# Four graph layers on one core: second layer with values stationary and probabilities scaled on GpSimd, and a changed order of work in the third and last layers

## The reference, cut to what matters

```python
h = maximum(layernorm(x), 0);  x = x + L0(h, adj, adj)   # attention, 8 heads of 32, eight masks, biases
h = maximum(layernorm(x), 0);  x = x + L1(h, adj)        # attention, 4 heads of 64, output bias only
h = maximum(layernorm(x), 0);  x = x + L2(h, adj)        # graph attention, 4 heads of 256, tanh, gated blend
h = maximum(layernorm(x), 0);  x = x + L3(h, adj)        # gated graph layer, 8 heads of 32, cosine links

def L1(x, mask):
    q, k, v = split_heads(x @ Wq), split_heads(x @ Wk), split_heads(x @ Wv)
    sim = where(mask, einsum('bhid,bhjd->bhij', q, k) / 8, -max)
    out = einsum('bhij,bhjd->bhid', softmax(sim), v)
    return merge_heads(out) @ Wo + bo

def L2(h, adj):
    Wh = einsum('bni,hoi->bhno', h, W) + bW
    A = tanh(where(adj, einsum('bhnp,bhmp->bhnm', einsum('bhno,hop->bhnp', Wh, attn), Wh), 0))
    ha = merge_heads(relu(einsum('bhnm,bhmo->bhno', A, Wh))) @ A_w.T
    hf = h @ fc_w.T
    c = sigmoid(hf @ g1_w.T + ha @ g2_w.T + gbias)
    return hf * c + ha * (1 - c)

def L3(x, m):                       # sm = mask, keep = not sm[..., 0:1]
    m = x @ map_w.T + map_b;  n = m by head / norm
    cos_adj = (n @ n.T * ~sm > 0.1)
    p = softmax(where(sm, -1e10, q @ k.T / sqrt(32))) * keep     # q, k from m
    adj = cos_adj * p
    return relu((adj @ sem) @ gcn_W.T / (adj.sum(-1) + 1))
```

## Time and profile before

| | |
|---|---|
| median of 3 runs | 2108.23 us (2107.6 to 2110.77) |
| the profiled execution | 2107.84 us, span 2106.0 us, granted PE clock 0.987 |
| PE busy | 2019.6 us (96%) |
| PE weight loads | 1865.0 us (89%), beside PE |
| DVE busy | 1486.2 us (71%) |
| ACT busy | 1019.4 us (48%) |
| POOL busy | 609.1 us (29%) |
| first, second, third, last layer | to about 385, 705, 1655, 2106 us |

### The profile page before, as it was taken

One profiled execution on the slowest core, in us unless ns is written; L12 is line 12 of the kernel. 1 busy time (PEld: TensorE's weight loads), 2 busy tenths in 40 slices (PEclk: granted clock), 3 DMA queues, 4 the chain that ended last, 5 costly groups with the idle time before them and its releaser, 6 DMA issues. The chain is left out here.

```text
span 2106.0 us, 52874 instructions
## 1 busy us (share of the span) xinstructions
PE 2019.6 (96%) x18448; PEld 1865.0 (89%) x18448; DVE 1486.2 (71%) x3280; ACT 1019.4 (48%) x2122; POOL 609.1 (29%) x656
## 2 busy tenths in 40 slices
PE   7999999899999799999999999999999899999998
PEld 7988888799999699999999999999998788888886
DVE  7999989577777455555555555555555599999998
ACT  6777777455555322322223223222222476776675
POOL 4545555322222011011111111111111344444443
PEclk9999999899999899999999999999999899999999
DMA  3222222433223200111111001110110122112221
GB/s 107 77 68 76 64 74 76 132 101 92 82 85 91 67 24 17 32 31 31 31 31 31 26 19 31 31 31 31 31 31 21 27 63 61 53 53 61 61 61 46
DMA packets 149370, 113.31 MB, mean 54 GB/s; under 512 B 42944, under 2 KB 148800, under 8 KB 149312
## 3 DMA queue, kind: packets, MB, share of 16 engines
q1 hardware_dynamic: 149312, 112.52, 18.3%
HBM read 78.93 MB, written 33.55 MB: 53 GB/s over the span
## 5 line engine op out<-in xcount | busy, mean ns | idle before, releaser
L274 POOL TENSOR_TENSOR ln_rstd<-ln_var_eps,minus_half 128x2 f32<-128x2 f32 x128 | 90.8, 709 | 760.4 <-DVE ln_var_eps L267 759.3
L1723 ACT ACTIVATE l_cat_hi<-banks 128x512 fp32r<-128x512 f32 x128 | 76.5, 598 | 260.2 <-PE banks L1894 260.2
L182 PE MATMUL banks<-ln_hT_hi,square_w_hi_held 128*128 128x256 f32 x512 | 153.2, 299 | 5.1 <-DVE square_w_lo_held L657 3.2
L291 ACT ACTIVATE ln_h<-ln_x,ln_shift,ln_rstd 128x256 f32<-128x256 f32 x256 | 139.1, 591 | 31.5 <-DVE ln_shift L281 26.8
L182 PE MATMUL banks<-ln_hT_hi,l_g_w_hi 128*128 128x256 f32 x512 | 148.8, 291 | 4.1 <-PEq L1992 4.1
L182 PE MATMUL banks<-l_cat_hi,l_aw_hi 128*128 128x256 f32 x512 | 144.5, 282 | 0.0
L183 PE MATMUL banks<-ln_hT_lo,square_w_hi_held 128*128 128x256 f32 x512 | 144.3, 282 | 0.0
L184 PE MATMUL banks<-ln_hT_hi,square_w_lo_held 128*128 128x256 f32 x512 | 144.0, 281 | 0.0
L184 PE MATMUL banks<-ln_hT_hi,l_g_w_lo 128*128 128x256 f32 x512 | 142.6, 278 | 0.0
L183 PE MATMUL banks<-ln_hT_lo,l_g_w_hi 128*128 128x256 f32 x512 | 142.5, 278 | 0.0
L183 PE MATMUL banks<-l_cat_lo,l_aw_hi 128*128 128x256 f32 x512 | 141.6, 277 | 0.0
(11 more groups left out here) (244 smaller groups left out, 6994.1 us busy)
## 6 DMA issues: line engine op xcount, KB each, us to landing
hidden<-y SPq DMA_DIRECT2D x96, 256.0 KB, 2.1
ln_x<-hidden SPq DMA_DIRECT2D x96, 256.0 KB, 2.7
x_res<-hidden SPq DMA_DIRECT2D x96, 256.0 KB, 2.9
ln_x<-x SPq DMA_DIRECT2D x32, 256.0 KB, 2.8
x_res<-x SPq DMA_DIRECT2D x32, 256.0 KB, 3.0
out<-y SPq DMA_DIRECT2D x32, 256.0 KB, 2.1
l_adj_u<-adj SPq DMA_DIRECT2D x96, 16.0 KB, 2.3
l_stage_attnT<-L_attnT SPq DMA_DIRECT2D x4, 256.0 KB, 3.2
```

The costliest lines, as they stand in the source:

```text
L182: nc.tensor.matmul(out, lhs(lh), rhs(rh), start=start, stop=False, skip_group_check=True)
L274: self.nc.gpsimd.tensor_tensor(self.rstd[:, g.slot], self.var_eps[:, g.slot], self.core.minus_half[:, 0:PAIRS], ALU.pow).then_inc(self.rst ...
L291: last = self.nc.scalar.activation(self.h[:, u, p, :], self.x[:, u, p, :], ACT.Relu, bias=self.shift[:, u, p:p + 1], scale=self.rstd[:, u, ...
L1723: nc.scalar.activation(cat_hi[:, h * KC:(h + 1) * KC], halves(B_HP[h]), ACT.Relu).then_inc(cat_hi_ready.sem, 1)
```

## The change

In the second layer the probabilities are scaled as in the first: DVE sums and inverts, POOL multiplies, PE transposes `weighted` and takes the values as the stationary operand, 128 columns wide, so the output transposes, `l_o` and the column of ones go. Here POOL's root is queued behind `weighted`; DVE's statistics come ahead of the softmax; PE's value projection is split around the transposes. In all layers the offset on line 267 becomes a `scalar_tensor_tensor` that takes the variance twice. In the third layer `Wh` is computed in units of 512 (two accumulations of 256), 256 and 260 columns, and `ha` in two halves in two banks. In the last layer DVE's order is another, POOL's mask comes last, and ACT applies the layer norm ahead of the second exponential.

```diff
@@ LayerNorm
+    def aggregate(self, dve, g, p):
+        u = g.slot
+        last = self.nc.vector.bn_aggr(self.mean_var[:, u, p, :], self.stats[:, u, p, :])
+        if p == PAIRS - 1:
+            last.then_inc(self.mean_var_ready.sem, 1)
+    def offset(self, dve, g):
         after(dve, self.mean_var_ready, g)
         after(dve, self.rstd_ready, g.back(2))
-        nc.vector.tensor_scalar(self.var_eps[:, u], self.mean_var[:, u, :, 1], LN_EPS, None,
-                                ALU.add).then_inc(self.var_eps_ready.sem, 1)
+        var = self.mean_var[:, u, :, 1]
+        self.nc.vector.scalar_tensor_tensor(out=self.var_eps[:, u], in0=var, scalar=LN_EPS, in1=var, op0=ALU.add,
+                                            op1=ALU.max).then_inc(self.var_eps_ready.sem, 1)
...
@@ attention_layer, POOL
-                if gn is not None:
+                if NT == 2 and gn is not None:
                     ln.root(pool, gn)
-                if direct and c2.exists(groups):
+                if c2.exists(groups):
                     for t in range(NT):
...
+                if NT == 1 and gn is not None:
+                    ln.root(pool, gn)
@@ attention_layer, DVE, one tile
+                    if gn is not None:
+                        ln.statistics(dve, gn, first=True)
                     if c2.exists(groups):
                         softmax_shift(0)
-                    if gn is not None:
-                        ln.statistics(dve, gn, first=True)
                     if e.exists(groups):
                         split_oT()
+                    if c2.exists(groups):
+                        weights_of_rows(0)
                     if gn is not None:
                         ln.statistics(dve, gn, first=False)
                         ln.shifts(dve, gn)
...
-                if not direct and c2.exists(groups):
-                    bank = ps[:, B_O:B_O + PAIRS, 0:heads * VW].rearrange("q p (h e) -> q p h e", h=heads)
...
@@ attention_layer, PE
-                if not direct and e.exists(groups):
-                    transpose_o()
                 if b1.exists(groups):
                     keys()
-                if not direct and c2.exists(groups):
-                    transpose_prob(prob, prob_ready, 0)
                 if e.exists(groups):
                     project_out()
                 if b1.exists(groups):
-                    values()
+                    values(range(PAIRS) if NT == 2 else range(1))
+                if c2.exists(groups):
+                    for t in range(NT):
+                        transpose_prob(t)
+                if NT == 1 and b1.exists(groups):
+                    values(range(1, PAIRS))
...
+                    for p in range(PAIRS):
+                        after(pe, probT_ready, c2, p // TP + 1)
+                        for b in range(2):
+                            for j in range(HH):
+                                r0, col = j * OUT_ROWS % P, j * OUT_ROWS // P * TOK + (2 * p + b) * S
+                                last = nc.tensor.matmul(
+                                    ps[r0:r0 + OUT_ROWS, B_OT, col:col + S], v_bd[:, u, p, b, j].rearrange("q a e -> q (a e)"),
+                                    probT[:, u, p // TP, (p % TP) * HH + j, b * S:(b + 1) * S], start=True, stop=True,
+                                    skip_group_check=True)
@@ graph_attention_layer
-    THIRDS = ((0, 320), (320, 384), (704, WC - 704))
+    UNITS = ((0, 512), (512, 256), (768, WC - 768))
-        B_HP, B_HA = (5, 6, 5, 6), 7
+        B_HP, B_HA = (5, 6, 5, 6), (7, 5)
...
-                    nc.scalar.activation(ha_hi[:], halves(B_HA), ACT.Copy).then_inc(ha_hi_ready.sem, 1)
+                    for c in range(KC):
+                        after(act, ha_in_psum, c2, c + 1)
+                        nc.scalar.activation(ha_hi[:, c], ha(c), ACT.Copy).then_inc(ha_hi_ready.sem, 1)
...
@@ gated_graph_layer, DVE (the calls alone)
                 softmax_shift(0); ln.statistics(dve, gn, first=True)
-                gate_output()                       # kept, den, r_den, factor, t
-                ln.statistics(dve, gn, first=False) # two aggregates, offset
-                softmax_shift(1)
-                ln.shifts(dve, gn)
-                n_bd copies; keep; sum_of_prob(0); m; sum_of_prob(1); link(0); link(1); norm_sq; norm_cl; y
+                gate_sums(); ln.aggregate(dve, gn, 0); gate_denominator(); ln.aggregate(dve, gn, 1)
+                gate_reciprocal(); ln.offset(dve, gn); gate_output()    # factor, t
+                ln.shifts(dve, gn)
+                softmax_shift(1)
+                n_bd copies; m; keep; link(0); norm_sq; norm_cl; link(1); sum_of_prob(0); sum_of_prob(1); y
@@ gated_graph_layer, ACT
-                    exponentials(1)
-                if gn is not None:
-                    ln.apply(act, gn)
+                if gn is not None:
+                    ln.apply(act, gn)
+                if c2.exists(groups):
+                    exponentials(1)
```

More of the change, by code:

```diff
@@ L508, in step @@
                 c2, e = g.back(2), g.back(3)
[L509 removed]
+                if low_on_pool and e.exists(groups):
                     after(pool, oT_hi_ready, e)
@@ L647, in step @@
                     ln.evacuate_hi(act, gn, B_HT)
-                if direct and b1.exists(groups):
+                if b1.exists(groups):
                     evacuate_v()
@@ L1204, in step @@
                     ln.root(pool, gn)
-                if g.exists(groups):
-                    after_dma(pool, adj_loaded, g)
-                    after(pool, scores_in_psum, g.back(2), apart=core)
-                    after(pool, keep_ready, g.back(2), apart=core)
-                    nc.gpsimd.tensor_scalar(mask[:, g.slot], adj_u8[:, g.slot], -MASKED, None,
-                                            ALU.mult).then_inc(mask_ready.sem, 1)
                 b1 = g.back(1)
@@ L1226, in step @@
                                             ALU.mult).then_inc(n_ready.sem, 1)
+                if g.exists(groups):
+                    after_dma(pool, adj_loaded, g)
+                    after(pool, scores_in_psum, g.back(2), apart=core)
+                    after(pool, keep_ready, g.back(2), apart=core)
+                    nc.gpsimd.tensor_scalar(mask[:, g.slot], adj_u8[:, g.slot], -MASKED, None,
+                                            ALU.mult).then_inc(mask_ready.sem, 1)
             run_steps(pool, step, groups, 1)
@@ L1369, in step @@
                 if e.exists(groups):
-                    gate_output()
-                if gn is not None:
-                    ln.statistics(dve, gn, first=False)
-                if c2.exists(groups):
-                    softmax_shift(1)
-                if gn is not None:
-                    ln.shifts(dve, gn)
+                    gate_sums()
+                if gn is not None:
+                    after(dve, ln.stats_ready, gn, apart=core)
+                    ln.aggregate(dve, gn, 0)
+                if e.exists(groups):
+                    gate_denominator()
+                if gn is not None:
+                    ln.aggregate(dve, gn, 1)
+                if e.exists(groups):
+                    gate_reciprocal()
+                if gn is not None:
+                    ln.offset(dve, gn)
+                if e.exists(groups):
+                    gate_output()
                 if c2.exists(groups):
@@ L1384, in step @@
                     last.then_inc(n_bd_dve_ready.sem, 1)
-                    after(dve, mask_ready, c2)
-                    after(dve, factor_steps, c2.back(2))
-                    nc.vector.tensor_scalar(keep[:, c2.slot], mask[:, c2.slot, :, 0], 1.0 / MASKED, 1.0, ALU.mult,
-                                            ALU.add).then_inc(keep_ready.sem, 1)
-                    sum_of_prob(0)
+                if gn is not None:
+                    ln.shifts(dve, gn)
+                if c2.exists(groups):
+                    softmax_shift(1)
                 if b1.exists(groups):
@@ L1396, in step @@
                 if c2.exists(groups):
-                    sum_of_prob(1)
-                if c2.exists(groups):
+                    after(dve, mask_ready, c2)
+                    after(dve, factor_steps, c2.back(2))
+                    nc.vector.tensor_scalar(keep[:, c2.slot], mask[:, c2.slot, :, 0], 1.0 / MASKED, 1.0, ALU.mult,
+                                            ALU.add).then_inc(keep_ready.sem, 1)
                     link(0)
-                    link(1)
                 if b1.exists(groups):
@@ L1787, in step @@
                     after(dve, gate_ready, e)
-                    nc.vector.tensor_tensor(diff[:], hf[:, e.slot], halves(B_HA), ALU.subtract).then_inc(blend_steps.sem, 1)
+                    for c in range(KC):
+                        last = nc.vector.tensor_tensor(diff[:, c], hf[:, e.slot, c], ha(c), ALU.subtract)
+                    last.then_inc(blend_steps.sem, 1)
                     after(dve, blend_steps, e, 1)
@@ L1793, in step @@
```

(11 more changed lines are left out.)

183 lines of the change are left out of this document (73 added, 110 removed).

## The result

The changed kernel took 2154.55 us (median of 4 runs, 2152.24 to 2158.32) against 2107.91 (2106.68 to 2110.77) for the kernel before: ratio 1.0219, interval 1.0204 to 1.0234, 46.6 us slower where 2111 us and a range to 2134 were predicted. The profiled execution took 2153.72 us, its span is 2151.3.

What follows compares the result with a forecast made beforehand. PE was taken to bound the second and third layers, with PE and DVE both near full in the first and last. From 2107.84 us, -18 + 31 - 12.5 + 3 = +3.5 gave 2111 us, range 2084 to 2134.

Steps and rivals of the forecast that it cites:

- Both rivals on the faster side: Second layer stays PE's, 2087 us, chance 0.15; last layer gains as PE's cosines come early enough, 2094 us, chance 0.18.
- If it no longer waits for POOL ... I take -18: First layer: the two-input offset no longer waits for POOL, so the layer keeps its early pace, -18 us.
- rival 1: The offset still waits for POOL: the first layer gains nothing and the second loses too, 2137 us, chance 0.11.
- Rival 1's second part: Second layer: the offset waits for `weighted` too, 0.3 us a group, +8 us.
- About 29 groups run at that pace: Second layer: about 29 groups at 10.5 us instead of 9.37, +33 us, taken as +31.
- loop over `y`, store, load, statistics: Second layer: closed loop from `y` through load, statistics, softmax, `weighted` and root back to `y`, 10.5 us per group.
- The rival of register waits: Both new chains have more separate wait instructions, 0.3 us a group in two layers, 2128 us, chance 0.14.
- 12 x 0.008 either way is 3 us: I take nothing: Third layer: the new unit widths add 12 matmuls a group, 3 us either way, counted as nothing.
- only `m` and `keep`, 0.7, remain to fill it: Last layer: DVE has 0.7 us of work in a 1.4 us wait for the cosines, so waits 0.7 to 0.8.
- inside the same time: Last layer: the wait of `norm_sq` for POOL's square lies within DVE's wait of 0.7 to 0.8 us.
- the predicted +3: Last layer: DVE's new order costs net 0.1 us a group, +3 us, bounds -17 and +8.

Runs made afterwards that it cites:

- halves_only: The kernel before with only the third layer's `ha` in two halves and two banks, units left at 320/384/324: ratio 0.9928, 2091.57 us.
- order_of_units: halves_only with the third layer's units reordered to 384, 320 and 324 columns: ratio 0.9967 against the kernel before.
- the best kernel: The kernel before with `ha` in halves, the last layer's new order with `link(1)` ahead, and the offset added by GpSimd: ratio 0.9816, 2071.47 us.

## Why the prediction was wrong

The sum was 2111, the measurement 2154.6. Of the 43 us between them the first layer has 17, the second 10, the third 9, the last 5; between 1 and 2 lie outside of the layers of the one profiled execution. Both rivals on the faster side fail: the second layer is not PE's alone (10.69 us a group), and the last layer gains nothing.

**First layer, the step that failed: "If it no longer waits for POOL ... I take -18".** It waits as before. The size of the wait was right (-21 us without it), and so was the steady pace (10.52 against 10.54). The row that it rested on the earlier trace rows shows VectorE beside a `pow` over 16 columns, not beside a full-width GpSimd multiplication or subtraction; where such an operation runs (189.25 above), the two-input form of two columns lasts until it ends. That is rival 1, given 0.11. The Trainium skill (GPSIMD Engine Reference, section "Specifications") states that VectorE instructions with two SBUF inputs contend for the SBUF interfaces that GpSimd shares with VectorE; the trace agrees beside `oT_lo` (1.23 us against 0.16), and does not beside the `pow` of the earlier trace rows (0.69 us, as without it). I set a row of another kind of neighbour against it and should have gone by the row nearest in kind, `oT_lo` itself in the earlier trace rows. The trace of the kernel before even held the new form itself beside a full-width neighbour. The shift is a `scalar_tensor_tensor` over two columns with its inputs in SBUF, and at the end of the second layer it took 1.25 us, where 0.15 is its median:

```profile
677.75 1.29 POOL L543 TENSOR_TENSOR l_x_bo<-x_res,l_bo_row 128x512 f32<-128x512 f32 x1
677.81 1.25 DVE L281 SCALAR_TENSOR_TENSOR ln_shift<-ln_mean_var,ln_rstd 128x2 f32<-128x2 f32 x1 [0.82 <-POOL ln_rstd L274]
```

Rival 1's second part, +8 us in the second layer, was wrong: the wait ends there when the queue in front of the root does.

**Second layer, the step that was too small: "About 29 groups run at that pace", +31 against +41.2.** The mechanism is as predicted: loop over `y`, store, load, statistics; PE waiting for `ln_h`; records of the value products 0.113 apart; PE's own work 9.66 where 9.6 was worked out. What was mis-sized: the loop is 10.69 and not 10.5 (it lay inside my bounds, as handovers of 0.04 each), and it holds all 31 distances between stores: 31 x 1.32 = 41, where I had taken 29 x 1.13 = 33 and rounded down to 31. And the prediction held the loop to be the only one; taking the load out of it gains only 0.18 us a group, the rest came when variance and root went ahead of the multiplication. The rival of register waits, 0.3 us a group, was not tested by itself; 9.66 against the 9.6 worked out leaves room for 0.06 in this layer.

**Third layer, the step that failed: "12 x 0.008 either way is 3 us: I take nothing".** The halves gained 12.4 us, as predicted. The units cost 9.4. The prediction looked at the products that were cut anew (which are 256 columns wide three times and 260 once, not 256 "fourfold"); but the distance of the products that were not touched rose from 0.113 to 0.118 us, which over 84 of them and 32 groups is enough for all of it. Why it rose stays open.

**Last layer, the step that failed: "only `m` and `keep`, 0.7, remain to fill it".** Between the copies and `link(0)` stand `smax` and `shifted` of the second tile too (rows above), so `link(0)` doesn't wait for the cosines. The excerpt of the change ahead of the prediction has this order wrong, and the prediction goes by it: it puts the copies of `n_bd` behind `ln.shifts` and `softmax_shift(1)`, while the changed kernel calls them ahead of both. The cost came from the wait of `norm_sq`, put down as lying "inside the same time", which now holds up the second `linked`. It was +3.6 us alone, so that the predicted +3 came out by luck there, and +8.0 in the change.

## What to carry to other kernels

Whether a small VectorE instruction waits for GpSimd is judged by rows with the same large neighbour. In this kernel the offset lasted until that neighbour ended, in either of its two forms, and giving it to GpSimd itself was the cure in the first layer, where that did not lengthen the chain. When a new operation is put into a loop over several engines, close every loop through it and take the longest, the second longest as well: the first mend only uncovers it. A change of several parts is worth taking apart even when the whole loses: here one piece, `ha` in halves, gained 12 us in its layer and was hidden under the units beside it. And an order of calls is read from the kernel that is built, not from an excerpt of it.

## What the hardware showed that I had not expected

A TensorE product of 256 columns came every 0.113 or every 0.118 us, in stretches of tens of products at a granted clock of 1.00 in both kernels. Which of the two it was changed with the widths and the order of the units ahead of them, for a reason that stays open: 10.6 us of the third layer between halves_only and order_of_units. Not every VectorE instruction beside a full-width GpSimd operation is held up. The offset is, in its one-input form too; a reciprocal that reads eight columns of SBUF isn't (0.20 us beside `l_weighted` in 30 groups, as without it):

```profile
194.28 2.04 POOL L520 TENSOR_TENSOR l_weighted<-l_prob,l_rz 128x512 f32<-128x512 f32 x2 [2.94 <-DVE l_rz L705]
194.82 0.20 DVE L705 RECIPROCAL l_rz<-l_z 128x8 f32<-128x8 f32 x1
```

In the rows of the best kernel GpSimd adds two columns in 0.20 us, idles 0.16 until its own next operation reads them, and takes 0.71 for the root of two columns.
